# A graph network kernel: two of sixteen row tiles in a cycle come from PE, not one

## The reference

```python
h = concatenate([x[row], edge_attr], axis=1)            # 53125 x 192
h = relu(batchnorm(h @ W1 + b1, g1, be1))               # 53125 x 128
s = segment_sum(h, col, n); cnt = segment_sum(1, col, n)
agg = where(cnt > 0, s / maximum(cnt, 1), 0)
h2 = concatenate([x, agg], axis=1)
h2 = relu(batchnorm(h2 @ W2 + b2, g2, be2))
x = layernorm(x + relu(h2 @ Wl + bl))
```

## Time and profile before

| what | value |
|---|---|
| time, median of 3 runs | 656.19 us (655.18 to 658.38) |
| profiled execution | 654.61 us, of which the profile's span is 652.9 us |
| busy in the span | PE 464.1, PEld 376.6, DVE 453.7, ACT 167.2, POOL 416.1 us |
| mean granted TensorE clock | 0.857 of full |
| gathers on POOL (L631) | 384 instructions, 945 ns the median |

### The profile page before, as it was taken

One profiled execution on the slowest core, in us unless ns is written; L12 is line 12 of the kernel. 1 busy time (PEld: TensorE's weight loads), 2 busy tenths in 40 slices (PEclk: granted clock), 3 DMA queues, 4 the chain that ended last, 5 costly groups with the idle time before them and its releaser, 6 DMA issues.

```text
span 652.9 us, 9532 instructions
## 1 busy us (share of the span) xinstructions
PE 464.1 (71%) x2687; PEld 376.6 (58%) x2687; DVE 453.7 (69%) x837; ACT 167.2 (26%) x414; POOL 416.1 (64%) x519
## 2 busy tenths in 40 slices
PE   4758777787777686666766657444445699999984
PEld 4527655565555565555655545322222699999674
DVE  4578776777676776776777777644555577777786
ACT  2211111111111111111111111111114366556475
POOL 5677777777777777777777777777777033333500
PEclk9798999878898988999788888855556599999998
DMA  7854444344444333444343334433224267777203
GB/s 194 280 174 133 134 117 115 99 125 133 133 133 133 111 105 105 119 121 117 119 118 112 81 97 117 117 117 117 70 80 122 60 191 235 226 229 223 60 2 98
DMA packets 47992, 84.35 MB, mean 129 GB/s; under 512 B 11913, under 2 KB 23480, under 8 KB 47831
## 3 DMA queue, kind: packets, MB, share of 16 engines
q1 hardware_dynamic: 28834, 47.19, 22.2%
q0 software_dynamic: 12672, 25.98, 16.9%
q10 hardware_dynamic: 6453, 10.79, 4.5%
HBM read 63.82 MB, written 20.08 MB: 129 GB/s over the span
## 4 chain that ended last, share of the span: by engine, by line
POOL 55%; issue 19%; PE 18%; DVE 4%; DMA 2%; ACT 1%; POOLq 0%; DVEq 0%; ACTq 0%
POOL res L631 40%; POOL work L631 14%; PE psH L838 7%; PE psC L838 7%; POOL res L613 1%; DVE res L1322 1%; DMA srci<-in_src 1%; DMA res<-in_x,srci 1%; PE psT L903 1%; PE psH L903 1%; DVE res L1324 0%; PE psT L819 0%; DMA work<-ytab,srci 0%; PE psH L755 0%; DVE agg L1313 0%
## 5 line engine op out<-in xcount | busy, mean ns | idle before, releaser
L631 POOL DMA_INDIRECT res<-ytab,srci x280 | 265.1, 947 | 86.5 <-issue 85.0
L727 PE MATMUL psH<-res,agg 125*128 125x128 f32 x1000 | 150.0, 313 | 39.1 <-DVE agg L1162 38.8
L727 PEld LDWEIGHTS psH<-res,agg 125*128 125x128 f32 x1000 | 142.6, 226 | 59.7 <-DVE agg L1162 57.7
L932 ACT ACTIVATE agg<-res 128x512 f32<-128x512 f32 x78 | 49.1, 630 | 294.1 <-DVE res L1153 197.1
L631 POOL DMA_INDIRECT work<-ytab,srci x104 | 99.1, 953 | 31.8 <-issue 31.4
L715 PE MATMUL psH<-w1e,work 128*128 128x256 f32 x200 | 65.8, 461 | 27.8 <-DVE res L1153 18.5
L1285 DVE TENSOR_TENSOR work<-res,psX 128x512 f32<-128x512 f32 x103 | 70.6, 687 | 21.4 <-PE psC L838 13.2
L656 POOL TENSOR_TENSOR agg<-agg,srci 128x64 f32 x104 | 32.2, 310 | 74.6 <-ACT srci L1014 74.4
L1162 DVE TENSOR_TENSOR agg<-res,psC 125x640 f32<-125x640 f32 x100 | 78.1, 813 | 0.9 <-PE psH L727 0.8
L715 PEld LDWEIGHTS psH<-w1e,work 128*128 128x128 f32 x200 | 42.3, 227 | 55.4 <-issue 37.5
L1177 DVE TENSOR_TENSOR psX<-agg,psX 128x512 f32<-128x512 f32 x103 | 71.0, 689 | 0.0
(11 more groups left out here) (195 smaller groups left out, 483.9 us busy)
## 6 DMA issues: line engine op xcount, KB each, us to landing
work<-in_edge_attr SPq DMA_DIRECT2D x26, 512.0 KB, 4.1
spill<-work SPq DMA_DIRECT2D x26, 256.0 KB, 2.5
res<-spill SPq DMA_DIRECT2D x25, 256.0 KB, 3.3
res<-ytab,srci POOLq DMA_INDIRECT x280, 2.6
hot_dram<-hotb ACTq DMA_DIRECT2D x13, 256.0 KB, 2.6
hot_dram<-work ACTq DMA_DIRECT2D x13, 256.0 KB, 2.2
hotb<-hot_dram SPq DMA_DIRECT2D x13, 256.0 KB, 2.7
work<-hot_dram SPq DMA_DIRECT2D x13, 256.0 KB, 3.1
```

The source lines that it names most:

```text
L631: pool.indirect_dma_start(rows[:, j * F:(j + 1) * F], None, ytab, bass.IndirectOffsetOnAxis(ap=srci[:, j, g:g + 1], axis=0)).then_inc(gath ...
L727: last = pe.matmul(psP[0][:, 0:F], nhot[n % 2][0:PN, (t - t0) * P:(t - t0 + 1) * P], ysb[0:PN, t * F:(t + 1) * F], start=False, stop=(t == ...
L932: act.activation(sq[g % 2], slot(i, i % 2, q), ACT.Square).then_inc(sq_ready, 1)
```

## The change

Group 2 of cycles 2 to 21 gets the same treatment as group 0, so POOL gathers 14 tiles a cycle, not 15, and DVE and PE do ten node pieces, not five, spread over the quarters as 3, 2, 3, 2. The source numbers of the 40 tiles take the same room as those of 20 did, since they are kept in bf16: ACT works out 25p - src once (bf16 holds the values 0 to -24, which are what is compared with) from int32 numbers that land where cycle 12's rows will stand; nodep holds -t in place of 25p + t. The cast and the wait for the load on DVE go; DVE waits for ACT's `srcz`. The count rows are placed at q = 0, not q = 1, and POOL's wait is one group looser.

```diff
+def node_groups():
+    return [(i, q) for i in range(ROWS0, ROWS1) for q in range(U) if q == 0 or q == 2]
...
-        NR = ROWS1 - ROWS0
-        srcb = tail(NR * P)
+        NODES = node_groups()
+        srcz = tail(len(NODES) * P // 2).bitcast(BF16)
...
+        NB5 = len(NODECUT)
+        NODEROWS = 12
+        srcn = res[:, NODEROWS * KEEP * GF:NODEROWS * KEEP * GF + len(NODES) * P]
...
-            return ROWS0 <= i < ROWS1 and q == 0
+            return (i, q) in NODES
...
-            sp.dma_start(srcb.bitcast(I32), src_rows.rearrange("k p -> (k p)").partition_broadcast(P)).then_inc(s_srcb, 16)
+            sp.dma_start(srcn.bitcast(I32), src_rows.rearrange("k p -> (k p)").partition_broadcast(P)).then_inc(s_srcb, 16)
...
-                    pool.wait_ge(h_ready, g - 2)
+                    pool.wait_ge(h_ready, g - 3)
...
-                    pool.wait_ge(nhot_used, len(NODECUT) * NR)
+                    pool.wait_ge(nhot_used, NB5 * len(NODES))
...
-                    if node_tile(i, 0):
-                        for b in ((0, 1), (), (2, 3), (4,))[q]:
-                            node_rows(i, b)
+                    node = (i, q // 2 * 2)
+                    if node in NODES:
+                        for b in ((0, 1, 2), (3, 4))[q % 2]:
+                            node_rows(*node, b)
...
+            act.wait_ge(s_srcb, 16)
+            act.wait_ge(s_node, 1)
+            act.activation(srcz[0:PN, :], srcn[0:PN, :].bitcast(I32), ACT.Identity, bias=nodeid[0:PN, 0:1], scale=-1.0
+                           ).then_inc(s_srcz, 1)
...
                 if node_tile(i, q):
-                    dve.wait_ge(nhot_used, len(NODECUT) * (i - ROWS0 + 1))
+                    dve.wait_ge(nhot_used, NB5 * (NODES.index((i, q)) + 1))
...
-                                  srcb[0:PN, k:k + P].unsqueeze(1).broadcast_to([PN, t1 - t0, P]),
+                                  srcz[0:PN, k:k + P].unsqueeze(1).broadcast_to([PN, t1 - t0, P]),
...
-                    if q == 1:
+                    if q == 0:
                         place_counts(i)
                         if i == 1:
                             keep_in_psum()
-                    if node_tile(i + 1, 0):
-                        if q == (1 if i == 1 else 0):
-                            dve.wait_ge(cnt_ps, i + 1)
-                        for b in ((0, 1), (), (2, 3), (4,))[q] if i > 1 else ((), (0, 1), (2, ), (3, 4))[q]:
-                            node_onehots(i + 1, b)
+                    node = (i + 1, q // 2 * 2)
+                    if node in NODES:
+                        for b in ((0, 1, 2), (3, 4))[q % 2]:
+                            node_onehots(*node, b)
...
-                dve.wait_ge(s_srcb, 16)
                 dve.wait_ge(s_node, 1)
                 dve.tensor_copy(iotap, iota[:, :])
-                dve.tensor_copy(nodep, nodeid[0:PN, :])
-                dve.tensor_copy(srcb[0:PN, :], srcb[0:PN, :].bitcast(I32)).then_inc(s_srcf, 1)
-                dve.wait_ge(s_srcf, 1)
+                dve.tensor_scalar(nodep, nodeid[0:PN, :], nodeid[0:PN, 0:1], -1.0, ALU.subtract, ALU.mult
+                                  ).then_inc(consts_kept, 1)
+                dve.wait_ge(consts_kept, 1)
+                dve.wait_ge(s_srcz, 1)
```

More of the change, by code:

```diff
@@ L213, in gnn_kernel @@
         nhot = [agg[:, H2 * P + k * 5 * P:H2 * P + (k + 1) * 5 * P] for k in range(2)]
+        NB5 = len(NODECUT)
+        NODEROWS = 12
+        srcn = res[:, NODEROWS * KEEP * GF:NODEROWS * KEEP * GF + len(NODES) * P]
         assert ROWS0 == 2 and ROWS1 * KEEP * GF <= TAB0 and H2 * P + 10 * P <= 3 * GF
+        assert NODEROWS * KEEP * GF + len(NODES) * P <= 18 * KEEP * GF
         def node_tile(i, q):
-            return ROWS0 <= i < ROWS1 and q == 0
+            return (i, q) in NODES
         negu = psX[:, 0:F].unsqueeze(1).broadcast_to([P, TILES, F])
@@ L233, in gnn_kernel @@
         s_srcb = sem("src_rows_spread")
-        s_srcf = sem("src_rows_as_float")
+        s_srcz = sem("src_rows_less_partition")
+        consts_kept = sem("constants_in_psum")
         nhot_ready = sem("node_onehots_ready")
@@ L719, in product, with node_rows @@
                     last.then_inc(prod_ready, 1)
-            def node_rows(i, b):
-                n = len(NODECUT) * (i - ROWS0) + b
+            def node_rows(i, q, b):
+                n = NB5 * NODES.index((i, q)) + b
                 t0, t1 = NODECUT[b]
@@ L726, in node_rows @@
                 for t in range(t0, t1):
-                    last = pe.matmul(psP[0][:, 0:F], nhot[n % 2][0:PN, (t - t0) * P:(t - t0 + 1) * P],
+                    last = pe.matmul(psP[q][:, 0:F], nhot[n % 2][0:PN, (t - t0) * P:(t - t0 + 1) * P],
                                      ysb[0:PN, t * F:(t + 1) * F], start=False, stop=(t == NT - 1))
@@ L1141, in make_h @@
                     return
[L1142 to L1146, removed]
+                tables = [m for m in range(par, i + 1, 2) if m or q >= EARLY]
+                dve.wait_ge(gathered[par][q], sum(16 * (TILES - node_tile(m, q)) for m in tables))
                 h = slot(i, par, q)
                 if node_tile(i, q):
-                    dve.wait_ge(nhot_used, len(NODECUT) * (i - ROWS0 + 1))
+                    dve.wait_ge(nhot_used, NB5 * (NODES.index((i, q)) + 1))
                     dve.tensor_tensor(h[:, F:GF], psP[q][:, F:GF], h[:, F:GF], ALU.add)
@@ L1153, in make_h, with node_onehots @@
                 dve.tensor_tensor(h, psP[q][:, :], h, ALU.add).then_inc(h_ready, 1)
-            def node_onehots(i, b):
-                n = len(NODECUT) * (i - ROWS0) + b
+            def node_onehots(i, q, b):
+                n = NB5 * NODES.index((i, q)) + b
                 t0, t1 = NODECUT[b]
@@ L1160, in node_onehots @@
                     dve.wait_ge(nhot_used, n - 1)
-                k = (i - ROWS0) * P
+                k = NODES.index((i, q)) * P
                 dve.tensor_tensor(nhot[n % 2][0:PN, :].rearrange("p (t e) -> p t e", t=t1 - t0),
-                                  srcb[0:PN, k:k + P].unsqueeze(1).broadcast_to([PN, t1 - t0, P]),
+                                  srcz[0:PN, k:k + P].unsqueeze(1).broadcast_to([PN, t1 - t0, P]),
                                   nodep[:, t0:t1].unsqueeze(2).broadcast_to([PN, t1 - t0, P]), ALU.is_equal
@@ L1453 @@
         'src': src.reshape(NG, P, TILES).transpose(1, 2, 0),
-        'src_rows': src.reshape(NG // U, U, P, TILES)[ROWS0:ROWS1, 0, :, 0],
+        'src_rows': np.stack([src.reshape(NG // U, U, P, TILES)[i, q, :, 0] for i, q in node_groups()]),
         'dst': dst.reshape(NG, P, TILES).transpose(1, 2, 0),
```

## The result

| | before | changed |
|---|---|---|
| median | 655.68 us (655.12 to 658.38, 4 runs) | 672.47 us (670.65 to 675.97, 4 runs) |
| profiled execution | 654.61 us | 670.65 us, span 668.9 |

The ratio is 1.0254, with a 95% interval of 1.0200 to 1.0308: slower (the interval's lower end is at 2.0%), 16.8 us by the medians, 16.0 by the profiled executions. 670 us was forecast.

What follows compares the result with a forecast made beforehand. Prediction: POOL's gathers bound the kernel before; DVE and PE in series take over. 65.4 + 10 x 20.0 + 9 x 19.4 = 440.0 against 425.9, +14.1 on 654.61 gives 668.7, plus 1.6 for the median: 670 us, range 655 to 685.

Steps and rivals of the forecast that it cites:

- POOL's part: POOL in cycles 2 to 21: one gather fewer a cycle saves 25.0 us, the dropped cast 0.9, 25.9 together.
- DVE's bare cycle: DVE's own work in one cycle without waits: 13.8 us before, 17.6 with five more node pieces, against POOL's 17.5.
- A piece: One node one-hot compare on DVE: 0.81 us alone, 0.735 from start to start, unchanged by the bf16 operand.
- the rival that bet on it: Node pieces on DVE: bf16 operand doubles the compare's speed, a piece takes 0.40 us, total 630 us; chance 5%.
- The turn: Third piece of quarters 0 and 2 starts 2.39 us after the first, against 1.47 unhindered: stall 0.92, at least 0.82.
- T+5.4: Quarter 0 with full x_product: PE has used the first piece 5.4 us after the first sum's end T; stall 1.5.
- Cycles: Intervals from (2,0) to (21,0): ten with full x_product at 20.0 us, nine without at 19.4.
- The rival about PE's clock: PE in the cycles: one slow ten-matmul loop each cycle at half clock adds 13.7 us, total 684 us; chance 12%.
- Start: Before cycle 2: index list lands at 40.5, ACT takes 4.8 us, sum of (2,0) starts at 64.6, ends 65.4.
- Where POOL meets DVE: First gather of cycle 22 waits for the sum of (21,0): near 440.0 against 425.9; earlier slack 12.0 us.

Runs made afterwards that it cites:

- the filler: Changed kernel plus two needless 512-column PE matmuls behind the first product of cycles 16 to 21; 668.11 us, ratio 1.019.
- the reordered kernel: Changed kernel, two buffers, first of three pieces placed before other sums of its quarter, x_product behind that piece's matmuls; 640.09 us, ratio 0.978.
- the fastest kernel: Changed kernel with a third one-hot buffer and the count rows back in quarter 1; 628.66 us, ratio 0.959.
- the fourth experiment: Kernel before with 14 gathers a cycle, tile 0 of group 2 in cycles 2 to 21 left out altogether; 629.4 us, ratio 0.960.
- the first, fifth and seventh: Changed kernel with a third one-hot buffer, 634.54 us; PE multiplying only each piece's last column of five, 650.81 us; third buffer and count rows in quarter 1, 628.66 us.

## Why the prediction was right

It named the place (DVE's third piece in quarters 0 and 2, waiting for a buffer that PE still reads), the engine that takes over, and the time: 670 us against 672.5. By its steps:

- **POOL's part**, 25.0 us for the gathers and 0.9 for the cast: 25.8 measured for the gathers by themselves. Of the 0.9 POOL kept 0.6, since the other slow gather of the start (1.56 us before, at 37.20) took 1.85.
- **DVE's bare cycle**, 17.6 us: 17.57 with three buffers and the count rows in quarter 1. As the change has it, it is 17.9, because the registers of the count rows are waited for 0.56 us at q = 0, not 0.27. This term I had taken as unmoved. With two buffers it costs nothing in quarter 0 of cycles with x_product, where it fills a wait.
- **A piece**, 0.81 us and 0.735 from one to the next: 0.815 and 0.73. The bf16 operand gained nothing, so the rival that bet on it fell. The perf-mode tier table in the Trainium skill's "VectorE: DVE Perf Modes" gives tensor_tensor its single rate with any operand in PSUM; this agrees.
- **The turn**, 2.39 us: 2.29 in quarter 2 at full clock (the lower bound given), 2.69 at half. In quarter 0 of cycles with x_product the third piece was forecast at T+5.4 and came at T+5.34. The stall ahead of it was forecast at 1.5 and is 1.0 (207.46 - 204.97 - 1.47), for the registers of the count rows had filled part of the same wait.
- **Cycles**: 19.74 us against 20.0 (ten), 20.0 against 19.4 (nine). In the first the stalls are 0.5 and 0.1 shorter than forecast and the bare cycle 0.3 longer; the second are long by the clock (0.6, which the filler gives back) and the count rows' registers. The rival about PE's clock was right for five of nineteen cycles (14 to 17 and 20), but not in its sign: the clock granted over cycles 12 to 20 is 0.95, not under 0.85, since only some of a cycle's matmuls are slow.
- **Start**: the sum of (2,0) began at 63.16, forecast 64.6. ACT could begin on the index list at 38.52, two us earlier than assumed, and took 4.55 us (4.8). The prediction put the lateness against 59.29 down to this list. With three buffers ACT begins on it at 38.27, just as late, and the sum starts at 59.43: the list delays PE's x_product (44.10), and it is the third piece, waiting 4.11 us for its buffer behind it, that passes this on. So the start's 3.9 us are the buffer's turn too.
- **Where POOL meets DVE**: one small step was wrong. The first gather of cycle 22 didn't wait for the sum of (21,0). POOL waits once a cycle, for the sum of quarter 1, and then runs: 428.56 + 11 x 1.249 = 442.3, 1.0 us behind the end of that sum. The slack before was 11.6 us and not 12.0, since the sum ended at 414.34; no other figure rests on it.

The sum: forecast +14.1; start -1.5, cycles with x_product -2.6, without +5.4, POOL +1.0 make 16.4; the trace has 16.35. Terms of opposite sign took each other's place in part, so the total is nearer than its parts.

What stays open: why the four register loads of the count rows end 0.3 us later behind quarter 0's sums than behind quarter 1's. The quarter alone isn't it: in the reordered kernel they stand in quarter 0 and are not late in cycles without x_product (0.26 at 376.92), and in the fastest kernel one of quarter 1's is late (0.62 at 207.36). What the index list, now twice as long, does to the other transfers of the first 40 us wasn't tried apart.

## What to carry to other kernels

When work goes from the bounding engine to two others that hand it to each other, their sum of busy time says too little: count the turn of each buffer (fill, handover, use, handover) and compare it with how far apart the fills n and n+2 stand in the program. Here both engines had room (over cycles 2 to 11 DVE is busy for 173 and PE for 181 of 197 us), and waits of 1.7 us in each cycle turned a 4% gain into a 2.5% loss. A third buffer gave all but 5 us of it back, and two buffers with the first fill moved ahead of one or two other instructions (and x_product moved on PE) nearly as much: 640.1 us against 634.5. Then place small fixed work by what it can fill: the same count rows belonged in the quarter with the stall while there was one, and elsewhere when it was gone.

## What the runs showed of the hardware

- Needless work can pay: two matmuls in a pause of PE cut three cycles by 0.6 us each and a fourth by 1.1, with the granted clock up from 0.95 to 0.99. Taking four fifths of the node rows' matmuls away let the granted clock fall from 1.00 and 0.95 to 0.61 and 0.54 and made a product 1.89 us, not 1.05.
- One matmul with 500 moving columns at a stride takes 1.94 us until the next product's start (203.31 to 205.25 here); one with 512 columns in a row takes 0.94 (two in 1.88). That it is the stride wasn't tried apart: the second also has 125 rows, not 128.
- The slow gather isn't tied to the cast alone. With the cast gone, the gather at 39.37 took 1.85 us beside the group one-hots of cycle 1 (L1142, 39.18, both inputs in SBUF); before, one at 37.20 took 1.56 beside the same instruction. In eight slow gathers beside such an instruction or the cast (two in the kernel before and two in the fourth experiment, one each in the changed kernel and the first, fifth and seventh) the gather ends 0.81 to 0.82 us behind the end of the DVE instruction, whenever it began: 39.37 + 1.85 against 39.18 + 1.22, and 37.20 + 1.56 against 36.72 + 1.22. Those of later cycles read one input from PSUM, and the gathers beside them take 0.94; so does the gather at 41.52, during ACT's conversion. The Trainium skill's "SBUF — State Buffer", Who interferes with whom, says that a DVE instruction with two SBUF inputs contends with a GpSimd instruction that reads SBUF; this agrees.
- A comparison of one bf16 operand in SBUF with a float32 one in PSUM runs at the speed of one with two float32 operands: 812 ns for 640 columns in the median, both.
